# The order of a step in the attention of layer 0: scores two steps ahead, transposes first

## The chip, the cores and the metric

The kernel runs on one core of one Trainium2 chip. The metric is the device time of one execution in microseconds (us). The engines are TensorE (PE, with its weight loads shown apart as PEld), VectorE (DVE), ScalarE (ACT), GpSimd (POOL) and SyncE (SP, which issues nearly all DMAs). Each runs its own list of instructions in order, and they meet through semaphores.

## The reference, cut to what matters

The program is two layers of a small network on 2 x 4096 tokens of width 256. Layer 0 is attention with one head of width 256 and a feed-forward block beside it, layer 1 a selective scan (the recurrence) with a mixture of experts. The change touches the attention of layer 0 alone:

```python
qkv = mix_precision_matmul(x, weight_qkv)       # x is the layer-normed input [2, 4096, 256]
q, k, v = jnp.split(qkv, 3, axis=-1)
q = q / jnp.sqrt(d)
qk = jnp.einsum('bqd,bkd->bqk', q, k)
s = jax.nn.softmax(qk, axis=-1)
y = jnp.einsum('bqk,bkd->bqd', s, v)
return jnp.matmul(y, out_w.T) + out_b
...
x = x + s * g                                   # g: the gate that the feed-forward block made before
```

## The kernel before, in words

The stages run one after the other with a fence between them, so that a stage ends when its slowest engine has ended: feed-forward of batch 0, attention of batch 0, feed-forward of batch 1, attention of batch 1, then layer 1.

Attention of a batch has `TILES` = 32 tiles of 128 queries, and each tile `KEY_CHUNKS` = 4 chunks of 1024 keys: `STEPS` = 128 steps per batch, 256 in all. It is an online softmax: a running maximum and an accumulator in SBUF that is rescaled at every chunk. Products of 32-bit quality are made of several cheaper ones, with a high and a low part of an operand (`_hi`, `_lo`). A step i has these parts:

- `scores(i, half)`: TensorE, 5 matmuls of 512 columns (L974 to L978) into one half of `scores[i % 2]`, two banks of PSUM. It waits until the exponential of step i-2 has read that buffer.
- `running_max(i)`: VectorE, a maximum over 1024 columns (L872) and a small one against the chunk before (L875, L878). It waits for both halves of the scores.
- `exponentials(i)`: ScalarE, the exponential with its sum (L1049) into `p[i % 2]`, and the correction factor (L1052). It waits for the maximum, and for the transposes of step i-2, which read the same `p`.
- `turn(i, half)`: TensorE, 4 transposes (L1000) of `p[i % 2]` into the bank `pt[half]`; then ScalarE copies it to `pt_hi` (L1058) and VectorE takes the rest to `pt_lo` (L884).
- `values(i, half)`: TensorE, 4 pairs of matmuls, `pt_hi` against the values (384 columns, L1012) and `pt_lo` (256 columns, L1013), into the single bank `ybank`. It waits for `pt_lo` of its half and until VectorE has taken the last step's sum out of `ybank`.
- `accumulate(i)`: VectorE, L892 or L898 and small operations up to L904.

Once a tile there is a `residual(t)` thread, of which each of the next four steps runs a piece between `values(i, 0)` and `values(i, 1)`: the division by the sum (L909, L912), two transposes (L1024, copies L1071 on ScalarE and L916 on VectorE), the output product of six matmuls (L1030 to L1032, L920), the gate and the residual on GpSimd (L947, L950), and the layer norm (L174, L176 on VectorE, L181, L184 on GpSimd, L198 on VectorE). GpSimd also splits a weight of the later stage each tile (L935, L937), with loads and stores of it on SP's queue. `queries` makes the queries of four tiles at once (L986 to L990, L1063, L864), in two pieces in two steps.

The order of all this is written out by hand in `attention_order`. Every engine goes through the same function with its own versions of the parts, and with `nothing` for those it has no share in; thus one edit there moves the instructions in the lists of TensorE, VectorE and ScalarE alike. SP and GpSimd pass only `residual`. The PSUM is full: one bank `misc`, four for the two score buffers, two for `pt`, one for `ybank`.

Of the kernel before, what the change touches and what calls it, by code (L numbers as in the profile page):

```python
# [70 lines left out]
def finish(thread):  # L71
    while True:
        try:
            next(thread)
        except StopIteration as e:
            return e.value
# [602 lines left out]
KEY_BLOCKS = KEYS // P  # L679
TILES = SEQ // P  # L680
STEPS = TILES * KEY_CHUNKS


class Attention(Stage):
# [74 lines left out]
def attention_order(b, scores, running_max, exponentials, turn, values, accumulate, queries, residual):  # L759


    first, last = b * STEPS, (b + 1) * STEPS - 1
    for band in range(DC):
        queries(b * GROUPS, band)
    scores(first, 0)
    scores(first, 1)
    running_max(first)
    exponentials(first)
    pending = None
    for i in range(first, last + 1):  # L770
        t, c = divmod(i, KEY_CHUNKS)
        if t % TILES + GT < TILES:
            if c == KEY_CHUNKS - 1 and t % GT == GT - 2:
                queries(t // GT + 1, 0)
            elif c == 0 and t % GT == GT - 1:
                queries(t // GT + 1, 1)
        if i < last:
            scores(i + 1, 0)
        turn(i, 0)
        if i < last:  # L780
            scores(i + 1, 1)
        turn(i, 1)
        if i < last:
            running_max(i + 1)
            exponentials(i + 1)
        values(i, 0)
        if pending is not None:
            next(pending, None)
        values(i, 1)
        accumulate(i)  # L790
        if c == KEY_CHUNKS - 1:
            if pending is not None:
                finish(pending)
            pending = residual(t)
    finish(pending)
# [10 lines left out]
def attention_sync(e, w, k, ffn, b, a, g_dram, x1_dram, xn_dram, w_dram):  # L806
# [12 lines left out]
    def residual(t):  # L819
# [22 lines left out]
        e.dma_start(xn_dram[rows, :], k.xn[:, :]).then_inc(k.s_xn, 16)  # L842

    attention_order(b, nothing, nothing, nothing, nothing, nothing, nothing, nothing, residual)
    if (b + 1) * TILES <= WEIGHTS:
        split_save((b + 1) * TILES - 1)
# [10 lines left out]
def attention_vector(e, w, k, ffn, wt, b):  # L857
# [48 lines left out]
    def residual(t):  # L906
# [18 lines left out]
        norm_apply_vector(e, w, k.ln, [x[:, :]], [k.xn[:, :]], t)  # L925

    attention_order(b, nothing, running_max, nothing, turn, nothing, accumulate, queries, residual)


def attention_gpsimd(e, w, k, consts, b):  # L930
    def split(r, half):
        raw, hi, lo = (t[r % 2][:, half * BANK:(half + 1) * BANK] for t in (k.w_raw, k.w_hi, k.w_lo))
        w.wait_ge(k.s_w_raw[r % 2], 16 * (r // 2 + 1))
        w.wait_ge(k.s_w_saved[r % 2], 32 * (r // 2))
        e.tensor_scalar(hi, raw, 1.0, 0.0, ALU.mult, ALU.add).then_inc(k.s_split, 1)  # L935
        w.wait_ge(k.s_split, 4 * r + 2 * half + 1)
        e.tensor_tensor(lo, raw, f32(hi), ALU.subtract).then_inc(k.s_split, 1)  # L937

    def residual(t):
        acc, x, n = k.acc[t % 2], k.x[t % 2], t // 2  # L940
        yield
        for half in range(2 if t < WEIGHTS else 0):
            split(t, half)
        yield
        w.wait_ge(k.s_biased, t + 1)
        w.wait_ge(k.s_g[t % 2], 16 * (n + 1))
        e.tensor_tensor(acc[:, :], acc[:, :], k.g[t % 2][:, :], ALU.mult).then_inc(k.s_gated, 1)  # L947
        w.wait_ge(k.s_gated, t + 1)
        w.wait_ge(k.s_x[t % 2], 32 * n + 16)
        e.tensor_tensor(x[:, :], x[:, :], acc[:, :], ALU.add).then_inc(k.s_x1, 1)  # L950
        yield
        norm_rstd_gpsimd(e, w, k.ln, consts, 1, t)

    attention_order(b, nothing, nothing, nothing, nothing, nothing, nothing, nothing, residual)


def attention_tensor(e, w, k, ffn, wt, kv, consts, b):
# [5 lines left out]
    def scores(i, half):  # L963
# [7 lines left out]
        w.wait_ge(k.s_exp, i - 1)  # L971
        if i % STEPS == 1:
            w.wait_ge(ffn.s_alpha, 2 * groups)
# [1666 lines left out]
class Combine(Stage):  # L2640


    def __init__(self, nc, ctx, sems, attn):
# [5 lines left out]
                (attn.s_x[1], 16 * BATCH * TILES), (attn.s_g[0], 8 * BATCH * TILES), (attn.s_g[1], 8 * BATCH * TILES)]  # L2649
        steps = BATCH * STEPS  # L2650
        used += [(attn.s_chunk_max, steps), (attn.s_max, steps), (attn.s_exp, steps), (attn.s_scaled, steps), (attn.s_acc, steps),
# [318 lines left out]
```

## Time and profile before

| what | value |
|---|---|
| time, median of 3 runs | 4765.51 us (4758.56 to 4766.25) |
| span of the profiled execution | 4756.4 us |
| attention of batch 0, first transpose to last value matmul | 185.36 to 1014.79 us |
| attention of batch 1, first transpose to last value matmul | 1206.40 to 2032.16 us |
| busy over the whole span | PE 86%, PEld 71%, DVE 73%, ACT 54%, POOL 54% |

The page gives the span of the profiled execution and no other time of it; the median of the runs lies 9.1 us above the span and the lowest run 2.2 us above. A matmul row's duration includes the time in which it drains while the next one already streams, so the duration is longer than the distance between two starts in a dense stream. Distances between starts are the measure of TensorE's time here. A weight load (PEld) has a row of its own.

### The profile page before, as it was taken

To read this page: it belongs to the slowest core of one execution; us is meant where nothing else is said; L and a number is where in the kernel's file an instruction comes from. 1 tells how busy PE (TensorE), PEld (TensorE's weight loads), DVE (VectorE), ACT (ScalarE), POOL (GpSimd) and SP (SyncE) were. 2 spreads that over 40 slices of the span, in tenths; PEclk is the share of its full clock that TensorE was granted. 3 is DMA by queue.
4 is the path that set the end of the run, shared out by engine and by line. 5 is a ranking of instruction groups with operands and counts; after the bars stand their busy time and mean duration, and the time that the engine had idled before them with its cause. 6 is when DMAs were issued, how large, how long until landed. Compare 5 with 4: busy or idle time off the path is not lost. (4 is left out here: it accounts for less than half of the span.)

```text
span 4756.4 us, 68001 instructions
## 1 busy us (share of the span) xinstructions
PE 4083.1 (86%) x24660; PEld 3380.9 (71%) x24660; DVE 3477.4 (73%) x4975; ACT 2579.2 (54%) x4869; POOL 2589.5 (54%) x1858
## 2 busy tenths in 40 slices
PE   8899999979999999978888866778888887888865
PEld 7788888858788888867777755656676666666653
DVE  5466666655566666626888889988888888888887
ACT  6544444437444444447576653256667666666655
POOL 3122222223122210026666656878999899999887
PEclk9999999989999999979999967889999999999996
DMA  2022222221122210024444431255655556556658
GB/s 90 19 97 76 85 86 76 88 87 41 52 89 73 88 58 20 22 68 141 148 143 140 141 112 60 81 173 167 192 178 179 176 186 188 173 172 190 188 164 315
DMA packets 271490, 572.90 MB, mean 120 GB/s; under 512 B 37169, under 2 KB 157746, under 8 KB 271154
## 3 DMA queue, kind: packets, MB, share of 16 engines
q1 hardware_dynamic: 246578, 534.98, 33.7%
q0 software_dynamic: 24576, 33.57, 3.9%
q8 instruction: 195, 3.19, 0.3%
q14 instruction: 141, 1.16, 0.1%
HBM read 445.64 MB, written 122.81 MB: 120 GB/s over the span
## 5 line engine op out<-in xcount | busy, mean ns | idle before, releaser
L1595 POOL TENSOR_TENSOR scan_drive_sb<-scan_b_wide_sb,scan_du_sb 128x1024 f32<-128x1024 f32 x512 | 1299.8, 2565 | 269.5 <-DVE scan_h_sb L1507 262.6
L1507 DVE TENSOR_TENSOR_SCAN scan_h_sb<-decay_bank,scan_state_sb,scan_drive_sb 128x512 f32<-128x512 f32 x896 | 1116.2, 1268 | 114.7 <-ACT decay_bank L1845 108.8
L1845 ACT ACTIVATE decay_bank<-scan_delta_sb,a_neg_sb 128x512 f32<-128x512 f32 x1024 | 701.0, 687 | 382.1 <-DVE scan_h_sb L1507 378.9
L1012 PE MATMUL ybank<-v_low_hi_lo_sb,pt_hi_b_sb 128*128 128x384 f32 x2048 | 665.6, 359 | 26.9 <-DVE pt_lo_b_sb L884 20.8
L1514 DVE TENSOR_TENSOR scan_ch_sb<-c_pair,scan_h_sb 128x1024 f32<-128x1024 f32 x512 | 614.2, 1200 | 63.6 <-PE c_pair L1682 63.3
L884 DVE TENSOR_TENSOR pt_lo_b_sb<-pt,pt_hi_b_sb 128x512 fp32r<-128x512 f32 x512 | 352.7, 690 | 420.1 <-ACT pt_hi_b_sb L1058 420.1
L1693 PE MATMUL y_bank<-identity_sb,scan_ch_sb 128*128 128x128 f32 x4096 | 652.2, 291 | 5.1 <-ACT scan_temp_sb L1863 5.1
L1693 PEld LDWEIGHTS y_bank<-identity_sb,scan_ch_sb 128*128 128x128 f32 x4096 | 546.2, 152 | 118.4 <-issue 19.1
L1682 PE MATMUL c_pair<-scan_cc_sb,select_state_sb 128*128 128x512 f32 x1024 | 387.1, 462 | 259.7 <-DVE scan_ch_sb L1514 259.0
L1049 ACT ACTIVATE p_b_sb<-scores,softmax_cols_b_sb 128x1024 f32<-128x1024 f32 x256 | 286.0, 1117 | 546.3 <-DVE softmax_cols_b_sb L878 409.1
L1013 PE MATMUL ybank<-v_low_hi_lo_sb,pt_lo_b_sb 128*128 128x256 f32 x2048 | 573.7, 280 | 0.0
L1058 ACT ACTIVATE pt_hi_b_sb<-pt 128x512 fp32r<-128x512 f32 x512 | 305.9, 598 | 414.7 <-PE pt L1000 414.7
L1012 PEld LDWEIGHTS ybank<-v_low_hi_lo_sb,pt_hi_b_sb 128*128 128x128 f32 x2048 | 385.0, 188 | 96.5 <-DVE pt_lo_b_sb L884 85.1
L1682 PEld LDWEIGHTS c_pair<-scan_cc_sb,select_state_sb 128*128 128x128 f32 x1024 | 178.4, 207 | 340.0 <-DVE scan_ch_sb L1514 327.2
L947 POOL TENSOR_TENSOR acc_b_sb<-acc_b_sb,g_in_b_sb 128x256 f32<-128x256 f32 x64 | 47.4, 741 | 628.8 <-DVE acc_b_sb L920 628.8
L1013 PEld LDWEIGHTS ybank<-v_low_hi_lo_sb,pt_lo_b_sb 128*128 128x128 f32 x2048 | 386.6, 189 | 0.0
L1000 PEld LDWEIGHTS pt<-identity_sb,p_b_sb 128*128 128x128 f32 x2048 | 241.1, 140 | 135.9 <-ACT p_b_sb L1049 90.1
L1000 PE MATMUL pt<-identity_sb,p_b_sb 128*128 128x128 f32 x2048 | 316.3, 277 | 15.6 <-ACT p_b_sb L1049 14.9
L2285 POOL TENSOR_TENSOR moe_h_lo_sb<-moe_g_sb,moe_h_hi_sb 128x512 fp32r<-128x512 f32 x192 | 283.2, 1475 | 82.6 <-ACT moe_h_hi_sb L2193 82.5
L872 DVE TENSOR_REDUCE softmax_cols_b_sb<-scores 128x1 f32<-128x1024 f32 x256 | 310.7, 1214 | 6.7 <-PE scores L978 6.7
L935 POOL TENSOR_SCALAR split_hi_sb<-split_raw_sb 128x512 fp32r<-128x512 f32 x102 | 63.5, 623 | 376.5 <-DMA split_raw_sb<-WgT 120.1
L2537 PE MATMUL layer_bank<-moe_xt_hi_sb,expert_hi_sb 128*128 128x512 f32 x512 | 228.2, 446 | 32.6 <-DVE moe_xt_lo_sb L2364 13.9
(328 smaller groups left out, 9898.6 us busy)
## 6 DMA issues: line engine op xcount, KB each, us to landing
scan_b_wide_sb<-b_scratch SPq DMA_DIRECT2D x512, 512.0 KB, 3.9
w_hi_scratch<-split_hi_sb SPq DMA_DIRECT2D x51, 512.0 KB, 2.8
w_lo_scratch<-split_lo_sb SPq DMA_DIRECT2D x51, 512.0 KB, 4.1
expert_hi_sb<-w_hi_scratch SPq DMA_DIRECT2D x48, 512.0 KB, 5.4
expert_lo_sb<-w_lo_scratch SPq DMA_DIRECT2D x48, 512.0 KB, 6.4
x_b_sb<-x SPq DMA_DIRECT2D x16, 512.0 KB, 4.0
split_raw_sb<-WgT SPq DMA_DIRECT2D x16, 512.0 KB, 5.5
x_res_b_sb<-x SPq DMA_DIRECT2D x64, 128.0 KB, 4.9
```

The costliest lines, as they stand in the source:

```text
L872: e.tensor_reduce(v[:, 0, c:c + 1], k.scores[i % 2][:, :], AX_X, ALU.max, negate=True).then_inc(k.s_chunk_max, 1)
L884: e.tensor_tensor(k.pt_lo[n % 2][:, :], k.pt[n % 2][:, :], f32(k.pt_hi[n % 2][:, :]), ALU.subtract).then_inc(k.s_pt_lo, 1)
L1000: turned = e.transpose(k.pt[n % 2][:, j * P:(j + 1) * P], k.p[i % 2][:, kb * P:(kb + 1) * P], consts.identity[:, :])
L1012: e.matmul(k.y_bank[:, 0:D + P], k.pt_hi[n % 2][:, cols], kv.v[:, block, :], start=(kb == 0), stop=False, skip_group_check=True)
L1013: last = e.matmul(k.y_bank[:, 0:D], k.pt_lo[n % 2][:, cols], kv.v[:, block, 0:D], start=False, stop=(kb == KEY_BLOCKS - 1), skip_group_che ...
L1058: e.activation(k.pt_hi[n % 2][:, :], k.pt[n % 2][:, :], ACT.Copy).then_inc(k.s_pt_hi, 1)
L1507: e.tensor_tensor_scan(k.h[i % H_BUFFERS][:, j, :], k.decay_banks[S % DECAY_BANKS][:, :], k.drive[i % DRIVE_BUFFERS][:, j, :], start, ALU. ...
L1514: e.tensor_tensor(k.ch[i % CH_BUFFERS][:, :, :], k.c_bank[:, :, :], k.h[i % H_BUFFERS][:, :, :], ALU.mult).then_inc(k.s_ch, 1)
L1595: e.tensor_tensor(k.drive[i % DRIVE_BUFFERS][:, :, :], k.b_wide[i % B_BUFFERS][:, :, :], k.du[c % 2][:, :].unsqueeze(1).broadcast_to([P, P ...
L1682: last = e.matmul(k.c_bank[:, j, :], wt.select[:, n:n + 1].broadcast_to([P, P]), k.cc[c % 2][:, :], start=True, stop=True)
L1693: last = e.matmul(k.y_bank[:, tokens], k.ch[i % CH_BUFFERS][:, j, tokens], consts.identity[:, :], start=(n == 0 and t == 0), stop=(n == ST ...
L1845: e.activation(k.decay_banks[S % DECAY_BANKS][:, :], k.delta[c % 2][:, :], ACT.Exp, scale=wt.a[:, n:n + 1]).then_inc(k.s_decay, 1)
```

## The change

A constant `LEAD = 2` takes the place of the lead of one step, and the transposes of a half come ahead of the scores that are issued beside them. Before, a step was: scores i+1 half 0, transposes i half 0, scores i+1 half 1, transposes i half 1, maximum and exponential i+1, values i half 0, residual piece, values i half 1, accumulate i. After, it is: transposes i half 0, scores i+2 half 0, transposes i half 1, scores i+2 half 1, maximum and exponential i+2, and the rest as before. Ahead of the loop stand the scores, maxima and exponentials of two steps instead of one. No instruction and no buffer is added or removed, and no wait is edited.

```diff
+LEAD = 2
...
-    scores(first, 0)
-    scores(first, 1)
-    running_max(first)
-    exponentials(first)
+    for i in range(first, first + LEAD):
+        scores(i, 0)
+        scores(i, 1)
+        running_max(i)
+        exponentials(i)
...
-        if i < last:
-            scores(i + 1, 0)
         turn(i, 0)
-        if i < last:
-            scores(i + 1, 1)
+        if i + LEAD <= last:
+            scores(i + LEAD, 0)
         turn(i, 1)
-        if i < last:
-            running_max(i + 1)
-            exponentials(i + 1)
+        if i + LEAD <= last:
+            scores(i + LEAD, 1)
+            running_max(i + LEAD)
+            exponentials(i + LEAD)
         values(i, 0)
```

## Rows read from the trace of the kernel before

**Rows 1.** Busy time by stretch, batch 0 and batch 1: engines, clock, DMA share, GB/s.

```profile
185.36:1009.26 823.90, 804.05 (x4630) 672.51 (x4631) 507.78 (x1114) 342.58 (x651) 181.97 (x240) 1.00 0.23 79
1206.40:2026.80 820.40, 804.33 (x4631) 673.25 (x4631) 503.99 (x1114) 342.77 (x651) 136.98 (x193) 1.00 0.17 57
```

**Rows 2.** Waits of TensorE's weight loads, batch 0: total us, times, longest.

```profile
PEld pt L1000 <- ACT p_b_sb L1049: 45.3, 90, 1.1
PEld ybank L1012 <- DVE pt_lo_b_sb L884: 42.5, 127, 2.7
```

**Rows 3.** The same waits, batch 1.

```profile
PEld pt L1000 <- ACT p_b_sb L1049: 42.8, 90, 2.0
PEld ybank L1012 <- DVE pt_lo_b_sb L884: 42.6, 127, 2.7
```

**Rows 4.** TensorE in order of time, one tile: start us, us, line, operation, [idle].

```profile
504.08 0.39 PE L974 MATMUL scores<-k_low_sb,q_hi_b_sb 128*128 128x512 f32 x1
...
508.73 0.38 PE L1024 MATMUL misc<-identity_sb,acc_b_sb 128*128 128x128 f32 x2
...
509.05 0.45 PE L1012 MATMUL ybank<-v_low_hi_lo_sb,pt_hi_b_sb 128*128 128x384 f32 x1
...
515.46 0.28 PE L1030 MATMUL misc<-vo_hi_sb,yt_hi_b_sb 128*128 128x256 f32 x1
...
516.14 0.33 PE L1012 MATMUL ybank<-v_low_hi_lo_sb,pt_hi_b_sb 128*128 128x384 f32 x1
...
518.45 0.60 PE L1000 MATMUL pt<-identity_sb,p_b_sb 128*128 128x128 f32 x4
518.80 0.48 PE L974 MATMUL scores<-k_low_sb,q_hi_b_sb 128*128 128x512 f32 x1
519.12 0.39 PE L975 MATMUL scores<-k_low_sb,q_lo_b_sb 128*128 128x512 f32 x1
...
519.82 0.40 PE L978 MATMUL scores<-k_hi_sb,q_lo_b_sb 128*128 128x512 f32 x1
520.05 0.60 PE L1000 MATMUL pt<-identity_sb,p_b_sb 128*128 128x128 f32 x4
...
520.86 0.33 PE L1012 MATMUL ybank<-v_low_hi_lo_sb,pt_hi_b_sb 128*128 128x384 f32 x1
...
521.60 0.28 PE L1013 MATMUL ybank<-v_low_hi_lo_sb,pt_lo_b_sb 128*128 128x256 f32 x1
522.07 0.44 PE L1012 MATMUL ybank<-v_low_hi_lo_sb,pt_hi_b_sb 128*128 128x384 f32 x1 [0.19 <-DVE pt_lo_b_sb L884]
522.34 0.28 PE L1013 MATMUL ybank<-v_low_hi_lo_sb,pt_lo_b_sb 128*128 128x256 f32 x1
...
524.25 0.39 PE L978 MATMUL scores<-k_hi_sb,q_lo_b_sb 128*128 128x512 f32 x1
524.62 0.66 PE L1000 MATMUL pt<-identity_sb,p_b_sb 128*128 128x128 f32 x4
...
529.57 0.39 PE L974 MATMUL scores<-k_low_sb,q_hi_b_sb 128*128 128x512 f32 x1
```

**Rows 5.** VectorE and ScalarE in order of time, the same tile, same columns.

```profile
508.92 1.21 DVE L872 TENSOR_REDUCE softmax_cols_b_sb<-scores 128x1 f32<-128x1024 f32 x1
...
510.71 1.12 ACT L1049 ACTIVATE p_b_sb<-scores,softmax_cols_b_sb 128x1024 f32<-128x1024 f32 x1 [2.44 <-DVE softmax_cols_b_sb L878]
...
511.82 0.28 ACT L1052 ACTIVATE softmax_cols_b_sb<-softmax_cols_b_sb 128x1 f32<-128x1 f32 x1
...
513.47 0.68 DVE L884 TENSOR_TENSOR pt_lo_b_sb<-pt,pt_hi_b_sb 128x512 fp32r<-128x512 f32 x1
...
521.32 0.69 DVE L884 TENSOR_TENSOR pt_lo_b_sb<-pt,pt_hi_b_sb 128x512 fp32r<-128x512 f32 x1 [0.92 <-ACT pt_hi_b_sb L1058]
521.93 1.21 DVE L872 TENSOR_REDUCE softmax_cols_b_sb<-scores 128x1 f32<-128x1024 f32 x1
...
526.03 0.68 DVE L884 TENSOR_TENSOR pt_lo_b_sb<-pt,pt_hi_b_sb 128x512 fp32r<-128x512 f32 x1
```

## The prediction

> **What bounds the kernel now.** I read the busy time by stretch first, because shares over the whole span mix stages. In the attention of layer 0, TensorE is busy 804 of 824 us at a granted clock of 1.00 (the 2.4 GHz level), VectorE 508, ScalarE 343, GpSimd 182, the DMAs at a share of 0.23 [rows 1]. So TensorE bounds these stages, and the reader is to see how little that busy time seems to leave: 20 us a batch. The second view, the waits of the weight loads, says more: 90 waits of transposes for the exponential, 45.3 us, and 127 waits of value matmuls for `pt_lo`, 42.5 us, nearly one a step [rows 2], and the same in batch 1 [rows 3]. These idle times overlap the drain of a matmul before, so they are no loss yet. The third view, TensorE in order of time, gives the loss from distances between starts.
>
> The Trainium skill, Perfetto Trace Analysis, section Identifying the Most-Contended Engine, says that matmul busy time is a poor measure of the distance to the bound, because matmuls are pipelined, and that the busy share of the weight loads is a good one. Here the two are 98% and 82% [rows 1]; by the first the change could bring at most 20 us a batch (my rival B), by the second up to 151. The distances below lie between, at some 70.
>
> **The change part by part.** It adds and removes no instruction. What it moves changes who waits.
>
> *Undisturbed lengths on TensorE.* Four transposes up to the next scores take 0.35 us (518.45 to 518.80). The five score matmuls take 0.32 + 0.70 + 0.23 = 1.25 (518.80, 519.12, 519.82, 520.05). A values half after a smooth entry takes 0.74 up to its last start and 0.12 to the next, with its first pair 1.15 in all (520.86 to 521.60 is three and a half pairs). A step of two of each is 0.70 + 2.50 + 2.30 = 5.50 us. I take 5.52, for the pair that crosses from scores to values [rows 4].
>
> *What a tile takes now.* From 504.08 to 529.57 it is 25.49 us [rows 4]. The residual pieces on TensorE are in it: the output product 0.68 (515.46 to 516.14), and two transposes some 0.43 (0.32 from 508.73 to 509.05, and 0.11 for the slow first pair after it) [rows 4]. In the new order a tile is 4 x 5.52 + 1.11 = 23.19. The difference is 2.30 us a tile, 0.57 a step. Two of its sources can be seen: before the transposes 0.37 where 0.23 is smooth (524.25 to 524.62), and before the second values half 0.47 where 0.12 is smooth (521.60 to 522.07) and 0.27 for its first pair where 0.17 is smooth (522.07 to 522.34) [rows 4].
>
> *Why the wait before values half 1 goes.* From the start of a transpose to the end of its `pt_lo` it takes 1.96 us (520.05 on TensorE; 521.32 + 0.69 on VectorE) [rows 4, 5]. Now only the last three transposes and values half 0 stand between, 0.4 + 1.15. After the change scores half 1 stands there too: 0.35 + 1.25 + 1.15 = 2.75, with 0.8 to spare. For half 0 the cover becomes 0.35 + 1.25 + 0.35 + 1.25 = 3.20.
>
> *Why the wait for the exponential goes.* With the scores of a step done, VectorE takes 1.21 for the maximum, and the exponential starts at most 1.79 after the maximum starts (508.92 to 510.71). The exponential and the correction take 1.40 (510.71 to 511.82 + 0.28) [rows 5]. Now the transposes want it after 4 us; after the change they want it a whole step later, nearly 10 us. It is then out of the question as TensorE's wait.
>
> *What is queued behind it, and is late next.* In ScalarE's list exponential i+2 stands ahead of both copies of step i+1; in VectorE's, maximum i+2, the residual piece and accumulate i stand ahead of `pt_lo` i+1. Count from the start T of a step. The scores i+2 are done at T + 3.2 and some 0.3 for the drain; the maximum starts at 3.55, the exponential at 5.3 at the latest, and the correction ends at 6.7. The next step's transposes start at T + 5.52 and are out 0.60 later, at 6.1, so the copy waits 0.6 for ScalarE; the copy (1.27 from the transposes' start to that of `pt_lo`, less their 0.60, so 0.67) and `pt_lo` (0.69) then end by 8.1, and values half 0 want it at 5.52 + 3.20 = 8.72. Slack 0.6. In the steps with residual work VectorE is the later one: from the start of the maximum to the start of the next `pt_lo` there are 4.55 us with the transposed output (508.92 to 513.47) and 4.10 with the layer norm (521.93 to 526.03) [rows 5]. That makes 3.55 + 4.55 + 0.69 = 8.79 against 8.72 + 0.43 for the longer step, and 8.34 against 8.72. So no step is late by this, though the margins are 0.4. `ybank` is free by then as well, for accumulate ends where `pt_lo` starts.
>
> *The ends of a batch.* The last two steps have no scores to cover `pt_lo`: each waits 1.96 less the two transposes' 0.7, some 1.25, where before one such wait and one for the exponential stood; and they take no part in the gain. At the start the first copies wait for exponential 1, some 0.6, while the 1.25 of a scores half moves into a wait that is there anyway. The longest wait for `pt_lo`, 2.7 [rows 2], comes from something else in ScalarE's queue and keeps most of its length. Together I charge 3 us a batch.
>
> *The clock, SP and GpSimd.* The clock is at its upper level in both stretches [rows 1] and TensorE's gaps get shorter, so I put nothing on it. SP's and GpSimd's lists don't change. Their work of a tile has 23.2 us instead of 25.5; GpSimd is busy 22% [rows 1].
>
> *The sum.* 32 x 2.30 = 73.6, less 3, is 70.6 a batch and 141 for both. The steps that make the queries aren't in the tile that I read; their matmuls are the same, but VectorE has one more copy in them on top of margins of 0.4. I take 6 off for them: 135 us. Bounds: the visible idle time alone, 20 + 16 = 36 from below [rows 1]; the weight loads' waits in full, 88 + 85 = 173, from above [rows 2, 3]; and below nothing if the late copies of rival D come about. The value is nearest to the distances, which measure the same engine. The stages are fenced, so what attention saves reaches the end. The sum is made against a span of 4756.4, and this becomes 4621; the median of the runs is 9 above the span, and there I expect 4765.5 - 135 = 4630 us.
>
> **The rivals.**
> A (the forecast): both waits go, TensorE runs a step in 5.5 to 5.6 us. 4630, its own range 4615 to 4660. Chance 0.78.
> B: only what shows as idle time of TensorE goes, since the rest is pipeline that refills after each change of work. 4765 - 36 = 4729. For it: the 98% [rows 1]. Against: undisturbed transitions of each kind are in the rows, at 0.23 and 0.12 [rows 4]. Chance 0.06.
> C: one wait goes and the other stays, because the copies sit behind the exponential. With the wait for `pt_lo` left, 42.5 us a batch stay [rows 2] and 2 x 28 = 56 are won: 4709. For it: slack of 0.4 in two of four steps. Chance 0.08.
> D, the other side: slower. The place is `pt_lo` half 0, behind exponential i+2 on ScalarE and maximum i+2 on VectorE. If that chain grows by more than its slack of 0.6 plus the 0.57 that a step gains, 1.2 us a step, the kernel becomes slower; a second exponential of 1.1 in the way, or a layer norm's wait in each step, would be such a thing. At 1.5 us it costs 2 x 128 x (1.5 - 1.2) = 80 us: 4845. Against: the order within these two lists is as before, only the index differs, and both engines have idle time (VectorE is busy 62%) [rows 1]. Chance 0.04.
> E: nothing happens, because the sum is bound elsewhere (a store or a split at the stage's end): 4765. Against: TensorE's row is dense up to the last step. Chance 0.04.
>
> **How the numbers follow.** The likeliest case gives 4630. The range 4608 to 4712 takes in A with an error of 20 below and case C, and leaves out B, D and E, 0.14, and a little of A's own spread. Faster by over 0.2% (9.5 us, about what a measurement of this kernel can tell from none) are A, B and C: 0.92. Within it E: 0.04; slower D: 0.04.
>
> **What would show it.** TensorE's weight loads wait for the exponential at most once or twice a batch, where 90 stood. The waits of L1012 for `pt_lo` fall from 127 to fewer than 20, and those left lie at the batch's ends and in the steps with two transposes (L1024). A tile, from one L974 to that of four steps on, takes 23.2 to 23.6 us. TensorE's busy share in the stretch hardly moves, while the weight loads' rises from 82% to about 89%. Attention of a batch, 829 and 826 us from the first transpose to the last value matmul, takes near 760. The copies L1058 wait less for transposes and start behind L1052. Layer 1 shows no change. I am wrong if the distance from the last score matmul to the first value matmul is over 0.3 in ordinary steps, if L1012 still waits once a step, or if the clock in rows like [rows 1] falls under 1.00.

## The result, and the profile after

The changed kernel takes 4623.98 us, the median of 4 runs (4622.09 to 4627.54), beside 4762.69 (4758.56 to 4766.25) before: a ratio of 0.9715, with a 95% interval of 0.9701 to 0.9729, so 136 us less by the ratio (139 by the medians). The profiled execution took 4625.5 us, its span is 4623.7. The forecast was 4630, the range 4608 to 4712.

The busy time by stretch, with the columns of [rows 1], for the attention of batch 0 and, below the dots, of batch 1:

```profile
186.79:949.00 762.21, 755.90 (x4650) 684.87 (x4650) 525.15 (x1123) 334.33 (x655) 183.65 (x244) 1.00 0.25 85
...
1142.59:1902.20 759.61, 754.06 (x4649) 683.35 (x4650) 522.91 (x1122) 334.35 (x655) 138.28 (x196) 1.00 0.19 62
```

Attention of a batch is 761.7 and 759.6 us long, from the first transpose (186.79 and 1142.59) to the start of the last value matmul (948.49 and 1902.20); it was 829.4 and 825.8. These differences, 68 and 66, are the whole gain: the two profiled spans differ by 132.7. What lies between the two batches is 2.5 us longer than before, and what follows to the end 2.7 us shorter. TensorE's busy share rose only from 98% to 99%, while the weight loads' rose from 82% to 90%.

The waits of the weight loads, batch 0 and below the dots batch 1, which answer to [rows 2, 3]:

```profile
PEld ybank L1013 <- DVE pt_lo_b_sb L885: 10.7, 14, 2.4
PEld pt L1001 <- ACT p_b_sb L1050: 0.8, 1, 0.8
...
PEld ybank L1013 <- DVE pt_lo_b_sb L885: 9.8, 11, 2.4
```

The 90 waits for the exponential became one, at the start, and the 127 for `pt_lo` became 14 and 11. The longest one, 2.7 before, has stayed: 2.4, in the second tile of each batch. Three more lie in the first step and the last two. The 10 and 7 others all lie in one place that the forecast did not name, ahead of the first values half in the step with the output product, which follows the step with the two transposes. A tile on TensorE, as in [rows 4] (`L1001` is the transpose, `L975` the first score matmul):

```profile
463.57 0.60 PE L1001 MATMUL pt<-identity_sb,p_b_sb 128*128 128x128 f32 x4
463.92 0.48 PE L975 MATMUL scores<-k_low_sb,q_hi_b_sb 128*128 128x512 f32 x1
...
469.76 0.60 PE L1001 MATMUL pt<-identity_sb,p_b_sb 128*128 128x128 f32 x4
...
475.38 0.60 PE L1001 MATMUL pt<-identity_sb,p_b_sb 128*128 128x128 f32 x4
...
480.90 0.60 PE L1001 MATMUL pt<-identity_sb,p_b_sb 128*128 128x128 f32 x4
...
486.69 0.60 PE L1001 MATMUL pt<-identity_sb,p_b_sb 128*128 128x128 f32 x4
```

From transpose to transpose four steps on it is 23.12 us (463.57 to 486.69), against 25.49 before. The plain step is 5.52 (475.38 to 480.90), the one with the output product 6.19, the one with the layer norm 5.62 and the one with the two transposes 5.79. The entry from transposes to scores is 0.35, as it was. VectorE and below the dots ScalarE, which answer to [rows 5]:

```profile
461.26 1.21 DVE L873 TENSOR_REDUCE softmax_cols_b_sb<-scores 128x1 f32<-128x1024 f32 x1
...
465.46 0.68 DVE L885 TENSOR_TENSOR pt_lo_b_sb<-pt,pt_hi_b_sb 128x512 fp32r<-128x512 f32 x1
...
473.25 1.21 DVE L873 TENSOR_REDUCE softmax_cols_b_sb<-scores 128x1 f32<-128x1024 f32 x1
...
477.34 0.68 DVE L885 TENSOR_TENSOR pt_lo_b_sb<-pt,pt_hi_b_sb 128x512 fp32r<-128x512 f32 x1
...
475.80 0.28 ACT L1053 ACTIVATE softmax_cols_b_sb<-softmax_cols_b_sb 128x1 f32<-128x1 f32 x1
476.01 0.60 ACT L1059 ACTIVATE pt_hi_b_sb<-pt 128x512 fp32r<-128x512 f32 x1
```

From the start of the maximum to the next `pt_lo` it is 4.20 us with the transposed output and 4.09 with the layer norm. The copy (L1059, 476.01) now stands right behind the correction (L1053, 475.80) on ScalarE: that is the wait that was moved out of TensorE's sight. The transposes of that copy began at 475.38, and its `pt_lo` ends at 478.02, 2.64 later, where the values want it 3.2 later.

Not every tile is like this one. In the tile two before it, the values of the step with the output product wait (VectorE, GpSimd, ScalarE, TensorE):

```profile
413.51 1.12 DVE L879 TENSOR_TENSOR softmax_cols_b_sb<-softmax_cols_b_sb 128x1 f32<-128x1 f32 x1
413.34 1.28 POOL L938 TENSOR_TENSOR split_lo_sb<-split_raw_sb,split_hi_sb 128x512 fp32r<-128x512 f32 x1
414.67 1.12 ACT L1050 ACTIVATE p_b_sb<-scores,softmax_cols_b_sb 128x1024 f32<-128x1024 f32 x1 [3.05 <-DVE softmax_cols_b_sb L879]
418.16 0.45 PE L1013 MATMUL ybank<-v_low_hi_lo_sb,pt_hi_b_sb 128*128 128x384 f32 x1 [0.23 <-DVE pt_lo_b_sb L885]
```

The small maximum against the chunk before (L879), 0.16 us in most steps, took 1.12. It ended at 414.63, and GpSimd's split of a weight (L938) ended at 414.62. All 39 of these small maxima that took over 0.3 us in this trace (of 256, up to 1.18) end within 0.02 us of a split (L936 or L938) that ran beside them; 11 others had a split beside them and stayed short. So the exponential began 2.41 us after the maximum (412.26 to 414.67), where the forecast has 1.79 at most. Of the 17 waits of this place, 16 follow a small maximum of 0.6 us or more. That GpSimd holds VectorE up is read from this coincidence; no run took GpSimd's work away.

The ends of a batch, TensorE, and the clock of the stretch in the last line:

```profile
936.47 1.03 PE L1001 MATMUL pt<-identity_sb,p_b_sb 128*128 128x128 f32 x8
939.51 0.44 PE L1013 MATMUL ybank<-v_low_hi_lo_sb,pt_hi_b_sb 128*128 128x384 f32 x1 [2.00 <-DVE pt_lo_b_sb L885]
...
941.96 0.52 PE L1013 MATMUL ybank<-v_low_hi_lo_sb,pt_hi_b_sb 128*128 128x384 f32 x1
...
944.09 1.13 PE L1001 MATMUL pt<-identity_sb,p_b_sb 128*128 128x128 f32 x8
946.20 0.44 PE L1013 MATMUL ybank<-v_low_hi_lo_sb,pt_hi_b_sb 128*128 128x384 f32 x1 [0.98 <-DVE pt_lo_b_sb L885]
...
941.00:944.00 3.00, 3.00 (x14) 3.00 (x14) 0.42 (x1) 0.00 (x0) 1.22 (x2) 0.50 0.00 0
```

The last step but one idles 2.00 us before its values (1.58 in batch 1), the last one 0.98 as before; I had charged 1.25 for each. It is so long because its copies (both halves, at 937.57 on ScalarE) stand behind the last exponential (936.02) and the copy of the transposed output (937.31). From 940.9 to 944.2 the granted clock is 0.50, the 1.2 GHz level.

### The profile page after: what moved, and what is told of

Read it like the earlier page. It is cut to its first block and busy times, and to the rows that moved or that the text cites. A ratio compares the mean times of both kernels' runs of the same rounds, so it can differ in the third digit from the quotient of the medians.

```text
span 4623.7 us, 68001 instructions
## 1 busy us (share of the span) xinstructions
PE 3964.4 (86%) x24660; PEld 3384.1 (73%) x24660; DVE 3508.3 (76%) x4975; ACT 2557.7 (55%) x4869; POOL 2586.6 (56%) x1858
## 5 line engine op out<-in xcount | busy, mean ns | idle before, releaser
L1694 PE MATMUL y_bank<-identity_sb,scan_ch_sb 128*128 128x128 f32 x4096 | 641.0, 288 | 5.6 <-ACT scan_temp_sb L1864 5.1
L1013 PE MATMUL ybank<-v_low_hi_lo_sb,pt_hi_b_sb 128*128 128x384 f32 x2048 | 625.8, 342 | 11.6 <-DVE pt_lo_b_sb L885 11.1
L1694 PEld LDWEIGHTS y_bank<-identity_sb,scan_ch_sb 128*128 128x128 f32 x4096 | 536.7, 150 | 117.3 <-issue 16.7
L1059 ACT ACTIVATE pt_hi_b_sb<-pt 128x512 fp32r<-128x512 f32 x512 | 303.9, 595 | 269.7 <-PE pt L1001 269.1
L1001 PE MATMUL pt<-identity_sb,p_b_sb 128*128 128x128 f32 x2048 | 305.9, 272 | 0.8 <-ACT p_b_sb L1050 0.8
L1001 PEld LDWEIGHTS pt<-identity_sb,p_b_sb 128*128 128x128 f32 x2048 | 250.0, 140 | 40.3 <-ACT p_b_sb L1050 1.7
L936 POOL TENSOR_SCALAR split_hi_sb<-split_raw_sb 128x512 fp32r<-128x512 f32 x102 | 63.1, 619 | 381.5 <-DMA split_raw_sb<-WdT 120.0
```

The lines of the kernel that those rows point to most:

```text
L1001: turned = e.transpose(k.pt[n % 2][:, j * P:(j + 1) * P], k.p[i % 2][:, kb * P:(kb + 1) * P], consts.identity[:, :])
L1013: e.matmul(k.y_bank[:, 0:D + P], k.pt_hi[n % 2][:, cols], kv.v[:, block, :], start=(kb == 0), stop=False, skip_group_check=True)
L1059: e.activation(k.pt_hi[n % 2][:, :], k.pt[n % 2][:, :], ACT.Copy).then_inc(k.s_pt_hi, 1)
L1694: last = e.matmul(k.y_bank[:, tokens], k.ch[i % CH_BUFFERS][:, j, tokens], consts.identity[:, :], start=(n == 0 and t == 0), stop=(n == ST ...
```

## The experiments

Each is compared with the kernel before on the same chip, and a difference in us is one of these ratios times 4763 us, unless it says otherwise. The changed kernel itself was run again with the last group (0.9712, 0.9699 to 0.9725).

**The two parts, one at a time.** First the order alone: the changed kernel with `LEAD = 1`.

```diff
-LEAD = 2
+LEAD = 1
```

> The changed kernel with a lead of one step: transposes first, scores i+1 beside them. Cover theory (a wait is the length of its chain less TensorE's work in between): the waits for pt_lo vanish, their cover is 2.75 us against 1.96; the wait for the exponential grows, for the scores end at T+3.5, the exponential at T+6.2, and the next transposes want it at T+5.5: 0.7 us in a plain step, 0.3 with the two transposes, none with the output product, so 1.7 us a tile and 64 x 1.7 = 109 above the changed kernel: about 4733. Rival L (the lead alone does it): no better than before, 4763. Rival O (the order alone does it): 4624.

Measured: 4737.08 us, ratio 0.9946 (0.9930 to 0.9963). Batch 0's waits, and TensorE in order of time:

```profile
PEld pt L1001 <- ACT p_b_sb L1050: 70.0, 90, 3.2
PEld ybank L1013 <- DVE pt_lo_b_sb L885: 2.9, 2, 1.7
...
508.73 0.39 PE L979 MATMUL scores<-k_hi_sb,q_lo_b_sb 128*128 128x512 f32 x1
...
511.95 0.65 PE L1001 MATMUL pt<-identity_sb,p_b_sb 128*128 128x128 f32 x4
...
518.17 0.66 PE L1001 MATMUL pt<-identity_sb,p_b_sb 128*128 128x128 f32 x4 [0.50 <-ACT p_b_sb L1050]
```

The waits for `pt_lo` are gone but two, and those of the transposes for the exponential take 70.0 us instead of 45.3 (3.2 of the 70.0 is the batch's first, ahead of the first transpose, which the 45.3 leaves out). From the last score matmul (508.73) to the next step's transposes (511.95) there is the time of all value matmuls and of the six of the output product, and there the wait is covered. The step behind it, with no work of TensorE's for the residual, idles 0.5 at its end (518.17). The time came as worked out: 110 us above the changed kernel, where 109 was expected. The split by steps did not quite: the step with the two transposes is 0.7 and 0.6 us longer (batches 0 and 1) than in the changed kernel, where 0.3 was expected.

Then the lead alone: `LEAD = 2` with the old interleaving.

```diff
+        if i + LEAD <= last:
+            scores(i + LEAD, 0)
         turn(i, 0)
         if i + LEAD <= last:
-            scores(i + LEAD, 0)
+            scores(i + LEAD, 1)
         turn(i, 1)
         if i + LEAD <= last:
-            scores(i + LEAD, 1)
             running_max(i + LEAD)
```

> A lead of two steps with the old interleaving (scores half 0, transposes half 0, scores half 1, transposes half 1). Cover theory: the wait for the exponential vanishes, the wait of values half 1 for pt_lo stays at about 0.45 us in plain steps, and the copies of half 0 come behind an exponential that starts late, because the maximum is queued behind pt_lo half 1: some 2.0 us a tile in all, 64 x 2.0 = 128 above the changed kernel, 4750 (4710 to 4780). Rival L: 4624. Rival O: 4763. If the two parts of the change simply added, this run's gain and that of the run with the order alone would add to 139.

Measured: 4745.22 us, ratio 0.9963 (0.9950 to 0.9976).

```profile
PEld ybank L1014 <- DVE pt_lo_b_sb L886: 65.9, 149, 3.6
...
513.71 0.44 PE L1014 MATMUL ybank<-v_low_hi_lo_sb,pt_hi_b_sb 128*128 128x384 f32 x1 [0.80 <-DVE pt_lo_b_sb L886]
```

No wait for the exponential is left, and there are more for `pt_lo` than before, 149 a batch. So each part alone brings 26 or 18 us, and together they bring 136: they don't add. Each removes one of two waits that stand in one loop, and the time that it frees goes into the other.

**Cover without a second step of lead.** The kernel before, lead of one, with both transposes ahead of the second half of the scores.

```diff
         turn(i, 0)
+        turn(i, 1)
         if i < last:
             scores(i + 1, 1)
-        turn(i, 1)
-        if i < last:
             running_max(i + 1)
```

> The kernel before with a lead of one, but both transposes ahead of scores half 1 (scores half 0, transposes half 0 and 1, scores half 1). Cover theory: pt_lo half 0 has 0.35+1.25+0.35 = 1.95 us of cover for 1.96, half 1 has more; the exponential ends at T+6.5 and is wanted at T+5.5+1.25 = 6.75. So nearly all waits go without a second step of lead: 4630 (4620 to 4650). Rival L (a lead of two is needed): 4763, or about the run with the order alone.

Measured: 4640.22 us, ratio 0.9750 (0.9732 to 0.9768), 17 us above the changed kernel.

```profile
PEld ybank L1011 <- DVE pt_lo_b_sb L883: 35.8, 128, 2.5
PEld pt L999 <- ACT p_b_sb L1048: 5.3, 9, 2.0
```

Nine waits for the exponential are left, and the ones for `pt_lo` half 0 are in each step but short, 0.28 us of the load's idle time on the mean, most of which lies under the drain of the score matmul: a plain step is 5.61 us long, 0.09 above the changed kernel's. The expectation that a lead of two isn't needed was right. The place of the last score matmuls, behind the transposes and ahead of the values, carries seven eighths of the gain.

**How much room the copies have.** One more copy on ScalarE in each step, between the wait for the maximum and the exponential.

```diff
         w.wait_ge(k.s_turned, 2 * (i - 1))
+        for _ in range(1):
+            w.wait_ge(k.s_pad, k.pads)
+            e.activation(k.pad[:, :], f32(kv.k_hi[:, 0:BANK]), ACT.Copy).then_inc(k.s_pad, 1)
+            k.pads += 1
         e.activation(k.p[i % 2][:, :], k.scores[i % 2][:, :], ACT.Exp, bias=v[:, 1, c:c + 1],
```

> The changed kernel with one more copy of 128x512 (0.6 us) on ScalarE in each of the 256 steps, between the wait for the maximum and the exponential; its output is not used. Cover theory: the least slack that the trace shows is 0.6, so nothing, 4624 to 4630. Rival D (the copies behind the exponential are already at their limit): up to 0.6 a step, 150 more.

Measured: 4648.15 us, ratio 0.9767 (0.9749 to 0.9786), so 25 us above the changed kernel. Somewhat wrong: not nothing, and a sixth of rival D's 150. In ordinary tiles all of it lies in the step with the output product, 6.57 and 6.53 us instead of 6.29 and 6.31 (batches 0 and 1; means of the 22 tiles of a batch that are neither its first two, nor its last, nor make queries).

```profile
PEld ybank L1016 <- DVE pt_lo_b_sb L888: 22.9, 33, 2.9
```

With two copies (`range(2)`):

> The same with two more copies (1.2 us) a step. Cover theory: only the step after the one with the two transposes is late, by 1.2 - 0.6 = 0.6 us, and the others just keep up: 64 x 0.6 = 38 above the changed kernel, 4662 (4640 to 4700). Rival D: 300 more.

Measured: 4708.80 us, ratio 0.9890 (0.9875 to 0.9905), 83 above. Wrong: twice what was expected, and a quarter of rival D. TensorE:

```profile
PEld ybank L1016 <- DVE pt_lo_b_sb L888: 62.5, 89, 3.6
...
505.17 0.40 PE L982 MATMUL scores<-k_hi_sb,q_lo_b_sb 128*128 128x512 f32 x1
...
512.17 0.44 PE L1016 MATMUL ybank<-v_low_hi_lo_sb,pt_hi_b_sb 128*128 128x384 f32 x1 [0.66 <-DVE pt_lo_b_sb L888]
```

and VectorE and, below the dots, ScalarE:

```profile
504.76 1.29 DVE L888 TENSOR_TENSOR pt_lo_b_sb<-pt,pt_hi_b_sb 128x512 fp32r<-128x512 f32 x2 [1.64 <-ACT pt_hi_b_sb L1066]
505.97 1.21 DVE L876 TENSOR_REDUCE softmax_cols_b_sb<-scores 128x1 f32<-128x1024 f32 x1
...
511.43 1.28 DVE L888 TENSOR_TENSOR pt_lo_b_sb<-pt,pt_hi_b_sb 128x512 fp32r<-128x512 f32 x2
...
504.15 1.07 ACT L1066 ACTIVATE pt_hi_b_sb<-pt 128x512 fp32r<-128x512 f32 x2
507.50 1.30 ACT L1055 ACTIVATE pad_b_sb<-k_hi_sb 128x512 f32<-128x512 f32 x2 [2.28 <-DVE softmax_cols_b_sb L882]
...
510.24 1.08 ACT L1066 ACTIVATE pt_hi_b_sb<-pt 128x512 fp32r<-128x512 f32 x2
```

The scores were done at 505.17 + 0.40, but the maximum starts at 505.97: it stands behind `pt_lo` of both halves (504.76, x2), whose copies (504.15, x2) stand back to back behind a late exponential. So the next maximum and exponential start late too, and in the following step the values wait 0.66 (512.17).

The place is the expected one: by the same means the step with the output product, behind the one with the two transposes, is 7.32 and 7.30 us long instead of 6.29 and 6.31, and the other three of a tile are together 0.2 longer. The size has two parts. Late in batch 1, where the small maximum stays at 0.16 us, that step is 7.0 instead of 6.20: 0.8 for 1.2 us of added work, so the slack was 0.4 and not 0.6. Where the small maximum is stretched beside GpSimd's splits, up to 1.28 us here, all of the stretch comes on top (8.1 in the longest plain case). So 0.6 us already cost something and 1.2 cost double.

The same copy in the kernel before:

> The kernel before with one more copy (0.6 us) of the same kind at the same place. Cover theory: there the exponential is TensorE's wait in 181 of 256 steps, so nearly each step pays it: 0.5 to 0.6 x 256 = 130 to 150, 4900. If ScalarE has slack in the kernel before too: 4763.

Measured: 4864.47 us, ratio 1.0220 (1.0204 to 1.0235), 105 above. The kernel before pays 0.41 of each 0.6, four times what the changed one pays.

```profile
PEld pt L1003 <- ACT p_b_sb L1056: 102.6, 114, 4.0
PEld ybank L1015 <- DVE pt_lo_b_sb L887: 43.8, 127, 2.7
```

The waits for the exponential went from 45.3 to 102.6 us in batch 0 (4.0 of it is again the batch's first), those for `pt_lo` stayed. The sign and the place are as expected; the size is a quarter under it, since the step in which the exponential was not waited for, the one with the output product, had some room: it grew by 0.27 us (6.49 to 6.76, by the same means), the others by 0.36 to 0.58.

Is it ScalarE's load or the place in its list? The two extra copies once more, ahead of the wait:

```diff
-        w.wait_ge(k.s_max, i + 1)
-        w.wait_ge(k.s_turned, 2 * (i - 1))
         for _ in range(2):
...
             k.pads += 1
+        w.wait_ge(k.s_max, i + 1)
+        w.wait_ge(k.s_turned, 2 * (i - 1))
```

> The changed kernel with the same two extra copies (1.2 us a step) on ScalarE, but ahead of the wait for the maximum instead of behind it. The run with them behind the wait took 1.1% of the time more than had been worked out for the changed kernel's slack. Queue theory: it is the place in the list that costs, since there the copies stand between a late maximum and the exponential and push the copies of both halves; ahead of the wait ScalarE idles 2.1 us and they cost nothing: 4624 to 4632. Rival (load: ScalarE's added work, or its reads beside TensorE, slows the step wherever it stands): 80 above, about 4705 as before.

Measured: 4622.63 us, ratio 0.9716 (0.9701 to 0.9730): no cost that these runs can tell (the changed kernel on the same chip has 0.9712). ScalarE:

```profile
502.02 0.60 ACT L1066 ACTIVATE pt_hi_b_sb<-pt 128x512 fp32r<-128x512 f32 x1 [1.00 <-PE pt L1004]
502.52 1.29 ACT L1053 ACTIVATE pad_b_sb<-k_hi_sb 128x512 f32<-128x512 f32 x2
504.71 1.12 ACT L1057 ACTIVATE p_b_sb<-scores,softmax_cols_b_sb 128x1024 f32<-128x1024 f32 x1 [0.90 <-DVE softmax_cols_b_sb L882]
...
506.00 0.58 ACT L1066 ACTIVATE pt_hi_b_sb<-pt 128x512 fp32r<-128x512 f32 x1
```

The copies (L1053, 502.52) fill the idle time between the second copy of a step (502.02) and the exponential (504.71), and the next `pt_hi` starts when it would. The same 1.2 us of work a step cost 83 us at one place and nothing that shows at the other.

**The longest wait that was left.** In the changed kernel, in the second tile of a batch, ScalarE runs the gates of the feed-forward with a table load, and the copies of both halves wait behind them. TensorE and its clock stand below the dots:

```profile
216.00 1.28 ACT L455 ACT_TABLE_LOAD   x1
217.30 2.00 ACT L455 ACTIVATE g_late_b_sb<-g_late_b_sb 128x1024 f32<-128x1024 f32 x2
219.21 1.06 ACT L1059 ACTIVATE pt_hi_b_sb<-pt 128x512 fp32r<-128x512 f32 x2
...
220.56 0.64 PE L1013 MATMUL ybank<-v_low_hi_lo_sb,pt_hi_b_sb 128*128 128x384 f32 x1 [1.98 <-DVE pt_lo_b_sb L885]
...
220.70:224.00 3.30, 3.30 (x13) 3.30 (x14) 1.70 (x3) 2.41 (x5) 0.00 (x0) 0.50 0.02 5
```

Behind the wait of 1.98 us the granted clock fell to 0.50, the 1.2 GHz level, so the place costs more than its wait.

The gates were moved ahead of the batch's first exponential:

```diff
     def exponentials(i):
         t, c = divmod(i, KEY_CHUNKS)
         v = k.cols[t % 2]
+        if i % STEPS == 0:
+            ffn0_gate_last(e, w, ffn, b)
         w.wait_ge(k.s_max, i + 1)
...
     def residual(t):
-        if t % TILES == GATE_TILE:
-            ffn0_gate_last(e, w, ffn, b)
         yield
```

> The changed kernel with the two gate activations of the feed-forward's last groups and their table load ahead of the batch's first exponential, where ScalarE idles 4.9 us, instead of in step 4, where TensorE waits 2.4 us for copies behind them. If that wait is theirs: it vanishes in both batches, 4624 - 5 = 4619. If the table loads at the start come onto the path: 4624 to 4630.

Measured: 4609.38 us, ratio 0.9689 (0.9676 to 0.9703), 12 below the changed kernel, more than was expected. ScalarE at the start of batch 0:

```profile
179.32 1.28 ACT L455 ACT_TABLE_LOAD   x1
...
182.63 1.28 ACT L1052 ACT_TABLE_LOAD   x1
185.53 1.11 ACT L1052 ACTIVATE p_b_sb<-scores,softmax_cols_b_sb 128x1024 f32<-128x1024 f32 x1 [1.62 <-DVE softmax_cols_b_sb L876]
```

The gates end, with the table back, at 183.91, and the exponential starts at 185.53 as it did: they are hidden. Whether 12 or 5 us are theirs was asked by running both again on one chip, the changed kernel first and then the one with the early gates.

> The changed kernel once more, to stand beside the next run on the same chip: 4624 (4618 to 4632).

Measured: 4619.27 us, ratio 0.9712 (0.9699 to 0.9725).

> The early gates once more beside the changed kernel. Their trace showed TensorE's wait of 2.4 us in step 4 gone in both batches, so 5 us are theirs; the other 7 of the 12 seen were a spell at 1.2 GHz at the end of batch 0 that fell elsewhere, and chance. If so: 5 below the changed kernel of the same call, 4619. If the gain is all theirs: 12 below.

Measured: 4616.17 us, ratio 0.9703 (0.9689 to 0.9716), 3 below the median of the changed kernel beside it, and the intervals overlap: whole times don't tell the gates' worth from nothing. The traces do. The second tile of a batch takes 26.92 and 26.93 us in the changed kernel, 26.92 and 25.38 in its second run, and 23.21, 23.21, 23.21 and 23.13 with the early gates. So the wait costs 2.2 us a batch, and the lower clock behind it another 1.5 in three cases of four; in the 25.38 the clock stayed at 1.00 behind a wait of 1.91. Of the first 12 some 7 lie in these two tiles. The rest lies elsewhere: the feed-forward between the batches, which the edit leaves alone, takes 190 us in some executions and 193 to 194 in others, of either kernel. The version with the early gates has the lowest times of the study, and by its traces it is the one to keep; what they show is 6 to 7 us in these two tiles together.

## Why the prediction was right

- *What bounds.* TensorE bounded the stage and its distances between starts gave the room, not its busy share. Rival B's 4729, from the idle time, is out by 105 us. The Trainium skill, Perfetto Trace Analysis, section Identifying the Most-Contended Engine, says to go by the share of peak arithmetic and the weight loads' busy share instead of the matmuls'; for the weight loads the traces agree, since the one went from 82% to 90% with the gain and the other only from 98% to 99%.
- *The undisturbed step.* 5.52 us was measured as 5.52. The tile, forecast at 23.19, was 23.12, and 23.2 on the mean. Its parts were off both ways: the two transposes cost 0.27 and not 0.43, and the layer norm's step, put at 5.52, is 5.62.
- *Both waits go.* Both went, for the reasons given: with the order alone only the one for the exponential stayed, with the lead alone only the one for `pt_lo`. Rival C in its own form, with the maximum and the copies behind each other, is what the lead alone does, and it costs 118 us more than both parts.
- *What is late next.* Forecast: 4.55 and 4.10 us from maximum to next `pt_lo`, measured 4.20 and 4.09. The margins were real but were read too well, from one tile: "the exponential starts at most 1.79 after the maximum starts" was 1.44 in most steps and up to 2.47 in the step with the two transposes, and 17 steps were late with no added work at all. They are no reserve that each step has anew, either, as the extra copies showed. Rival D's mechanism exists. Lateness begins at some 0.4 us of added work in the step with the least room, where I had read 0.6; the gain was not lost at 1.2, as I had put it, for only one step of four pays much, and there the kernel was still 52 us faster than before.
- *The ends.* Charged at 3 us a batch. The last step but one was worse than charged, by 0.75 and 0.33 us, the last one better by 0.27. The last tile as a whole went from 23.8 and 23.4 us to 23.6 and 21.6, so in batch 1 it gained nearly what other tiles did, and in batch 0 the lower clock took 1.5 us of that. The first transposes came 1.4 us later than before (186.79 against 185.36).
- *The sum.* 70.6 a batch before the charge for the query steps, 68 and 66 measured. The 6 us taken off for both batches were about right in size by luck, and wrong in place. The tiles that make queries gained most, 2.4 and 2.2 us (means of 7 tiles: 27.8 and 27.6 before, 25.4 and 25.3 after). The ordinary tiles gained 2.1 and 2.0 instead of 2.30 (means of 22: 25.34 and 25.27 before, 23.22 and 23.23 after). The mis-sized term is the tile that was read before: its 25.49 lies 0.2 above the mean of its kind.
- *The rest of the program.* Nothing changed there beyond 3 us, as forecast.

## What to carry to other kernels

Price a wait by the chain's length less the work that its waiter has in between, and look for the loop in which several waits stand: taking one out alone moves its time to the next (26 and 18 us for the parts, 136 for both). Before deepening a pipeline, try where in the step its independent work stands; one block of matmuls between a producer and its consumer gave 119 of the 136 us with no second step of lead. Put spare work of an in-order engine ahead of its wait, if it idles there for long enough, and not behind it (0 against 83 us here for the same instructions). Read a margin from many steps before you count on it: here one small instruction of 0.16 us took up to 1.18 in some of them.

## What the runs showed of the hardware

A small VectorE instruction (128x1) took 0.16 us in most steps and up to 1.18 beside GpSimd's splits of 128x512, and then ended with the split, within 0.02 us, in all 39 cases of over 0.3 us in the changed kernel's trace. In 11 cases it ran beside a split and stayed short; what tells them apart is open.

The granted clock fell from 1.00 to 0.50 within attention behind single waits of TensorE, though it had been 1.00 for some 710 us before the one at 941. In the changed kernel that was behind idle times of 1.98 us (second tile, both batches) and behind eight transposes and 2.00 us (end of batch 0), and in its second run behind 1.91 us. It stayed at 1.00 behind 1.91 us in that run's batch 1, behind 1.58 at the end of the changed kernel's batch 1, and behind 1.82 at the end of batch 0 with the early gates. Each fall cost some 1.5 us: the second half of the value matmuls took 2.13 us (941.96 to 944.09) instead of 1.15, and the matmuls just ahead of it were slower too.
